# State-space units of a four-block sequence kernel: the exponent products move between the two halves of the gate's products

## The reference

```python
proj = hidden_states @ in_proj_w.T
gate, xBC, dt = jnp.split(proj, [INTER, INTER + CONV_DIM], axis=-1)
...
x, Bm, Cm = jnp.split(xBC, [INTER, INTER + NG * SS], axis=-1)
y = _ssd(x.reshape(Bsz, S, NH, HD), Bm.reshape(Bsz, S, NG, SS), Cm.reshape(Bsz, S, NG, SS), D, dt, dt_bias)
y = y.reshape(Bsz, S, INTER)
yg = y * jax.nn.silu(gate)
...
# inside _ssd, per chunk of 128 tokens and head h
cs = jnp.cumsum(dA, axis=-1)
seg = cs[..., :, None] - cs[..., None, :]
Lmat = jnp.where(tri, jnp.exp(seg), 0.0)
scores = jnp.einsum('bclhn,bcshn->bchls', Cc, Bc) * Lmat
Ydiag = jnp.einsum('bchls,bcshp->bclhp', scores, xdt)
```

## Time and profile before

| | |
|---|---|
| median of 3 runs | 2188.53 us (2187.5 to 2189.29) |
| profiled execution, whole time | 2190.99 us |
| profiled execution, first to last instruction (span) | 2188.9 us |
| PE busy | 2121.9 us, 97% |
| DVE busy | 1721.2 us, 79% |
| ACT busy | 1239.7 us, 57% |
| mean granted clock of PE | 0.987 |

### The profile page before, as it was taken

The page is one execution under the profiler, slowest core; times in us unless marked ns, Lnnn a source line. Parts: engine busy times, 40 slices in busy tenths (PEclk is TensorE's granted clock), DMA queues, the critical chain, the costliest instruction groups (busy, mean ns, idle before and its releaser), DMA issues. The chain is left out here.

```text
span 2188.9 us, 35859 instructions
## 1 busy us (share of the span) xinstructions
PE 2121.9 (97%) x10933; PEld 1691.8 (77%) x10933; DVE 1721.2 (79%) x2943; ACT 1239.7 (57%) x2216; POOL 688.5 (31%) x419
## 2 busy tenths in 40 slices
PE   9999999989999999999999999999999999988997
PEld 7888778868777777777777777777777777766775
DVE  7554446468778888898888888888888888888886
ACT  3222225433377677677767767677777767753232
POOL 5644334311122323324233333324233333330000
PEclk9999999999999999999999999999999999999999
DMA  5312404123231212222132122222221221212433
GB/s 191 113 51 87 159 7 138 58 55 114 98 102 51 91 52 67 73 69 68 49 92 61 55 78 64 68 64 77 61 71 58 68 83 49 74 38 97 144 123 108
DMA packets 126578, 176.40 MB, mean 81 GB/s; under 512 B 17748, under 2 KB 83796, under 8 KB 126068
## 3 DMA queue, kind: packets, MB, share of 16 engines
q1 hardware_dynamic: 126452, 175.07, 25.6%
HBM read 165.72 MB, written 9.31 MB: 80 GB/s over the span
## 5 line engine op out<-in xcount | busy, mean ns | idle before, releaser
L72 PE MATMUL bank<-xT_hi,C_w_hi 128*128 128x512 f32 x1160 | 473.6, 408 | 7.9 <-POOL C_w_lo L1658 7.5
L73 PE MATMUL bank<-xT_lo,C_w_hi 128*128 128x512 f32 x1160 | 459.9, 396 | 0.0
L74 PE MATMUL bank<-xT_hi,C_w_lo 128*128 128x512 f32 x1160 | 459.8, 396 | 0.0
L1658 POOL TENSOR_TENSOR C_w_lo<-C_raw,C_w_hi 128x512 fp32r<-128x512 f32 x130 | 180.5, 1389 | 789.6 <-ACT C_w_hi L1752 746.2
L1365 DVE SCALAR_TENSOR_TENSOR C_acc<-bank,C_par,C_acc 128x510 f32<-128x510 f32 (+2 forms) x384 | 281.2, 744 | 60.4 <-ACT C_acc L1712 37.7
L1481 DVE TENSOR_TENSOR C_decay<-C_decay,C_cb 128x512 f32<-128x512 f32 x384 | 291.9, 789 | 4.8 <-ACT C_decay L1838 4.8
L72 PEld LDWEIGHTS bank<-xT_hi,C_w_hi 128*128 128x128 f32 x1160 | 220.4, 190 | 62.7 <-POOL C_w_lo L1658 8.8
L74 PEld LDWEIGHTS bank<-xT_hi,C_w_lo 128*128 128x128 f32 x1160 | 220.1, 190 | 51.7
L73 PEld LDWEIGHTS bank<-xT_lo,C_w_hi 128*128 128x128 f32 x1160 | 220.9, 190 | 45.3
L72 PE MATMUL bank<-C_out_hi,C_yg_hi 128*128 128x512 f32 x512 | 202.1, 395 | 7.4 <-DVE C_yg_lo L1451 4.0
L74 PE MATMUL bank<-C_out_hi,C_yg_lo 128*128 128x512 f32 x512 | 201.3, 393 | 0.0
(11 more groups left out here) (268 smaller groups left out, 4326.8 us busy)
## 6 DMA issues: line engine op xcount, KB each, us to landing
C_raw<-in_Cxg SPq DMA_DIRECT2D x65, 512.0 KB, 3.6
C_cs_second<-cs_rows SPq DMA_DIRECT2D x64, 512.0 KB, 4.7
C_raw_out<-in_Cout SPq DMA_DIRECT2D x64, 256.0 KB, 2.8
ahead_raw<-in_D SPq DMA_DIRECT2D x32, 512.0 KB, 3.6
front_raw<-in_A SPq DMA_DIRECT2D x20, 512.0 KB, 4.3
B_stat_raw<-in_D SPq DMA_DIRECT2D x16, 512.0 KB, 3.6
ahead_raw<-in_D SPq DMA_DIRECT2D x32, 256.0 KB, 2.6
cb_rows<-C_decay SPq DMA_DIRECT2D x8, 768.0 KB, 3.2
```

Of the source, the lines that this page charges most:

```text
L72: pe.matmul(out, lh, rh, start=start, stop=False)
L73: pe.matmul(out, lh, rl, start=False, stop=False)
L74: return pe.matmul(out, ll, rh, start=False, stop=stop)
L1658: e.tensor_tensor(w_lo[:, slot, :], raw_at, f32(w_hi[:, slot, :]), ALU.subtract).then_inc(lo_done, 1)
```

## The change

The exponent products of both halves come behind the first half of the gate in all units but unit 0. In the seven `group_ended` units the second half's stays where it is, and the first half's joins it.

```diff
@@ body(u) on PE
                     inside(u)
                 if u.group_ended:
                     squares_sum(u)
+                in_g(u, 0)
                 if not u.first:
                     seg(u, 0)
-                    if not u.group_ended:
-                        seg(u, 1)
-                in_g(u, 0)
-                if u.group_ended:
                     seg(u, 1)
                 in_g(u, 1)
                 if u.first:
```

## The result

| | before | after |
|---|---|---|
| median of the runs | 2188.2 us (2186.13 to 2190.31, 14 runs) | 2190.42 us (2189.38 to 2194.53, 14 runs) |
| ratio of the times, with its 95% interval | | 1.0016 [1.0009, 1.0023] |
| profiled execution, whole time and span | 2190.99, 2188.9 us | 2192.94, 2190.7 us |
| first product of unit 1 to that of unit 63 | 1316.03 us | 1320.28 us |
| a regular unit (median of 40) | 20.93 us | 21.03 us |

The ratio stands for +3.5 us, where +3.8 was forecast.

What follows compares the result with a forecast made beforehand. PE, busy 97% of the span, was taken as the bound; 41 units x 0.10 us, +4.1 (to +4.5), with -0.5 for closing units gave +3.8 on 2188.53, so 2192.3 us; range 2187.8 to 2194.2.

Steps and rivals of the forecast that it cites:

- PE as the bound: In the 64 units PE sets the pace, busy 298.56 of 300 us; starting other engines earlier wins nothing.
- no cost at ScalarE: At the exponentials L1838: pairs come 2.8 us later against 6.0 us of cover, so ScalarE loses nothing.
- The joint behind the blocks: PE from the last block group to the second gate product: 0.64 us with an exposed fp32r load, 1.13 before.
- The middle joint: PE between the gate's halves, where the pairs now stand: 1.05 us instead of 0.46 in a regular unit.
- The units that pay: 41 of 56 units pay 0.10 us each, +4.1; 14 units and unit 1 absorb it in PE's waits.
- The closing units: Seven units that close a group: joints 3.10 us instead of 3.17, -0.07 each, -0.5 us in all.
- Rival 1: fp32r load behind the blocks hidden: fully, 2184.7 us, chance 6%; only its last 0.09, 2188.0 us, 7%.
- Rival 2: PE's waits for `C_yg_lo` don't absorb the cost; all 56 units pay, +5.7, 2194.2 us; chance 8%.
- Rival 3: Exponentials on ScalarE become late; needs a delay above 6.0 us, each unit then pays the excess; chance 1%.
- the first joint: From blocks to gate on PE: a skill's rule would hide the fp32r load; the forecast took it as exposed.

Runs made afterwards that it cites:

- e2: Changed kernel with both exponent pairs behind the whole gate, ahead of the output tiles; ratio 1.0028.
- e6: Changed kernel with both exponent pairs behind the gate and two of the four output tiles; ratio 1.0036.
- after_again: The changed kernel, unaltered, measured a second time; 2191.66 us, ratio 1.0015.
- e9: Kernel before the change with one more bf16 product of 512 columns behind the squares in the seven closing units; 2188.82 us, ratio 0.9999.
- e4: Kernel before the change, with the last exponent pair ahead of a gate product cut into three so that a long product comes last; ratio 1.0003.
- e7: e4 with PE's inner loop over three pairs of units instead of two, its outer loop a third shorter; 2185.91 us, ratio 0.999.
- e5: Changed kernel with the second exponent pair cut as in e4, long product last, ahead of the gate's second half; ratio 0.9995.
- e3: Changed kernel with one more bf16 product of 512 columns between blocks and gate in the 56 regular units; ratio 1.0058.
- e1: Changed kernel with one exponent pair back behind the blocks, the other between the gate's halves, from unit 1 on; ratio 1.0016.

## Why the prediction was right, point by point

- PE as the bound, and the change as a matter of PE's order alone: right. No engine's waits got a new line in the stage.
- No gain from a later pair or an earlier gate half, no cost at ScalarE: right. Of 6.4 us from the second pair to its reader 3.4 are left; e2 stretched the delay to 5.7 us without a wait, e6 to 8.4 with one.
- The joint behind the blocks, 0.64 us, from two pairs of neighbours that the trace did show: 0.65 measured. The middle joint, 1.05: 1.06. The difference of a regular unit, +0.10 to 0.11: +0.10 (20.933 to 21.033, medians of 40).
- The units that pay, 41: right in number (units 3 to 8, 11 to 15 ... 59 to 63), 41 x 0.10 = 4.1 us; 40 of them lie in the stage's 4.25 us and make 4.0 of it. The six units that begin a group behind the second (16, 24 ... 56) took 21.61 to 22.07 us after and 21.66 to 22.00 before; together they took 130.98 and 130.62 us, and 130.55 in `after_again`, so what they add is scatter.
- The closing units, -0.5 us: wrong twice. The step that failed was the joint from squares to gate, taken from the transposes with their hidden load (0.35 us): it took 0.43, so such a unit is 0.03 longer instead of 0.07 shorter, +0.2 instead of -0.5 in the seven. The transposes stream 128 columns a record and the squares one; that a record of one column covers less of the load is my reading, which no run tested. And a gain there would hardly have counted: units 25 and 26 are one stretch of 44.1 us with VectorE's pace, as e9 showed, before the change and behind it. I had applied that reasoning to unit 26 and not to the one ahead of it. So the term should have been about nothing.
- Rival 1, the hidden load: fell; the load starts 0.32 us behind the last block group, in the row. Rival 2, no absorption: fell in units 10, 18 ... 58. Rival 3, late exponentials: fell; by e2 and e6 it begins between 5.7 and 8.4 us of delay.
- Rule and row at the first joint: the Trainium skill, TensorE: Matmul & The Clock Gate, section Step-by-step: what each phase is for, would have the load pulled ahead; the trace does not agree behind the blocks, where PE's weight queue stands idle for 0.17 us. The Trainium skill, TensorEngine Tiling (Array Packing), section Key Properties, says that a change of tiling mode drains the engine; the same row agrees with it, though no run separates a drain from another cause of the 0.17 us.
- The size of the result: +3.8 forecast, +3.5 by the ratio, +4.4 by the trace of the stage including unit 63 (1336.93 to 1341.29 us from the first product of unit 1 to the last transpose). That 3.8 lies so near to 3.5 is in part luck: without the closing units' -0.5 the sum is +4.1 to +4.5, nearer to the trace, and the ratio's interval, +2.0 to +5.0 us, cannot tell the two.

## What to carry to other kernels

On an engine that streams without a gap, a reordering is priced at the joints: list the neighbours before and after, read each pair's distance of starts from the nearest rows, and count the weight loads that no long product covers. In this kernel a product of few columns, and a switch from half-array to full-array products, left the next load bare; a long product put last ahead of the fp32r load took back 0.07 to 0.11 us a unit (e4, e7, e5). Check then where PE waits anyway, since a cost or gain ahead of a stop that another engine times does not reach the end.

## What the runs showed of the hardware that was not expected

- With one more product a unit in PE's loops, PE stopped at the beginning of the outer loop in some rounds (e3, e4), for 1.2 to 2.6 us by the distance of starts, with 41 and 48 transfers of the instruction queue instead of 37 and a transfer just ahead of the end of each stop; e5, with one product less than e4 in each closing unit, had none. With a loop a third shorter there were 33 and no stop. The stage took 1318.62 us with the stops and 1312.34 without, by that alone.
- Two stops of 2.4 and 2.3 us, 0.7 us of work apart (e4, unit 32), were followed by a granted clock of 0.50 and steps of up to 0.43 us instead of 0.23, at a price of 2.4 us, as much as one of the stops. Behind the three single stops, with 0.9 to 1.2 us of idle time (e3, e4), the clock stayed at 1.00.
- A bf16 load behind an fp32r product starts only when that product has streamed (0.24 us behind its start, at 1210.56), whereas an fp32r load behind an fp32r product overlaps it (the load for the product of 1210.32 starts at 1210.09, with the product before). It costs little, since the bf16 load is short: 0.24 to the pair against a step of 0.23.
- The fp32r load is worth 0.07 to 0.11 us when bare, in five kernels: 0.10 behind the blocks, 0.09 in e1, 0.08 to 0.09 in e3, 0.07 in e4, 0.09 to 0.11 in e5.
